# A segmented maximum and minimum in one 256-wide step, and straight code for the column loop of a graph network

## The reference, cut to what matters

```
for l in range(3):
    msg = concat([h[src], h[dst]]) @ Mw.T + Mb         # per edge, with self loops
    s1, s2 = segment_sum(msg, dst), segment_sum(msg * msg, dst)
    mx, mn = segment_max(msg, dst), segment_min(msg, dst)
    mean = s1 / deg
    var = relu(s2 / deg - mean * mean)
    std = sqrt(var + 1e-30)
    agg = concat([mx, mn, std, var])
    u = concat([h, agg, agg * (log(deg + 1) / 4), agg * (4 / log(deg + 1))]) @ Uw.T + Ub
    # batch norm, a product with mix_w, leaky relu, + h, layer norm, elu
```

## Time and profile before

| | |
|---|---|
| median of three runs | 3951.08 us (3942.02 to 3959.58) |
| the profiled execution | 3915.32 us |
| its span | 3913.5 us |
| mean granted TensorE clock | 0.785 |
| busy: PE, PEld, DVE, ACT, POOL | 63%, 35%, 57%, 18%, 32% |
| instructions in the trace | 50857 |
| bytes moved by DMA | 511.54 MB, mean 131 GB/s |

### The profile page before, as it was taken

The page is one execution under the profiler, slowest core; times in us unless marked ns, Lnnn a source line. Parts: engine busy times, 40 slices in busy tenths (PEclk is TensorE's granted clock), DMA queues, the critical chain, the costliest instruction groups (busy, mean ns, idle before and its releaser), DMA issues. The chain is left out here.

```text
span 3913.5 us, 50857 instructions
## 1 busy us (share of the span) xinstructions
PE 2472.3 (63%) x11996; PEld 1384.5 (35%) x11997; DVE 2233.6 (57%) x6995; ACT 692.3 (18%) x1557; POOL 1258.7 (32%) x1321
## 2 busy tenths in 40 slices
PE   6988879886968955455456654454448644544563
PEld 2444345743635532222224422222225322222242
DVE  6877766463353265555555645555556645555555
ACT  0235532411121030000001500000003300000112
POOL 3000000002000036666642155655640356555520
PEclk8999989997979977677678676766767867767785
DMA  3122366253523535444441144444430444444411
GB/s 109 50 93 109 142 210 230 99 206 124 176 81 138 176 100 179 159 163 159 138 145 40 53 160 144 160 155 135 157 113 1 141 136 160 154 134 158 153 43 45
DMA packets 152225, 511.54 MB, mean 131 GB/s; under 512 B 32194, under 2 KB 51552, under 8 KB 151248
## 3 DMA queue, kind: packets, MB, share of 16 engines
q1 hardware_dynamic: 94782, 350.03, 25.5%
q0 software_dynamic: 43536, 93.43, 8.6%
q10 hardware_dynamic: 13826, 67.12, 4.2%
HBM read 280.33 MB, written 230.13 MB: 130 GB/s over the span
## 5 line engine op out<-in xcount | busy, mean ns | idle before, releaser
L615 POOL DMA_INDIRECT rows_g<-a_dram,idx_now x1173 | 1133.3, 966 | 1566.8 <-DMA a_dram<-g 801.4
L1485 PE MATMUL psum<-hs,slab 128*128 128x384 bf16 x6600 | 1196.2, 341 | 166.2 <-issue 124.0
L1485 PEld LDWEIGHTS psum<-hs,slab 128*128 128x128 bf16 x6600 | 674.5, 102 | 711.2 <-issue 326.3
L1045 DVE SCALAR_TENSOR_TENSOR run<-run,mask_pt,rows_g 128x128 f32<-128x128 f32 x1170 | 405.6, 347 | 278.5 <-issue 224.7
L1048 DVE SCALAR_TENSOR_TENSOR run<-run,mask_pt,rows_g 128x128 f32<-128x128 f32 x1170 | 403.3, 345 | 34.6 <-issue 26.8
L1637 PE MATMUL psum<-identity,std_now 128*128 128x128 f32 x75 | 33.6, 448 | 598.1 <-ACT std_now L1341 512.9
L1432 PE MATMUL psum<-onehot_key,onehot_lane 128*128 128x512 bf16 (+1 forms) x1968 | 366.4, 343 | 60.9 <-issue 36.3
L726 DVE TENSOR_SCALAR onehot_key<-key_row,key_at 128x1600 bf16<-128x1600 f16 x492 | 310.2, 630 | 0.0
L1644 PE MATMUL psum<-w_U,vturned 128*128 128x384 f32 x150 | 119.2, 896 | 292.6 <-ACT vturned L1349 265.2
L1341 ACT ACTIVATE std_now<-var_now,eps 128x128 f32<-128x128 f32 x75 | 30.1, 401 | 1444.5 <-DVE var_now L1007 928.9
L1432 PEld LDWEIGHTS psum<-onehot_key,onehot_lane 128*128 128x128 bf16 x1968 | 160.4, 100 | 249.5 <-issue 55.0
(11 more groups left out here) (298 smaller groups left out, 3018.2 us busy)
## 6 DMA issues: line engine op xcount, KB each, us to landing
slab<-at_part SPq DMA_DIRECT2D x200, 800.0 KB
scan_dram<-run SPq DMA_DIRECT2D x291, 512.0 KB
at_part<-part_now ACTq DMA_DIRECT2D x50, 800.0 KB, 3.6
sums_dram<-run ACTq DMA_DIRECT2D x43, 576.0 KB, 2.9
rows_g<-a_dram,idx_now POOLq DMA_INDIRECT x1173
rows_g<-in_attr SPq DMA_DIRECT2D x43, 148.5 KB
a_dram<-g SPq DMA_DIRECT2D x3, 1600.0 KB, 7.7
agg<-sel_dram SPq DMA_DIRECT2D x3, 1600.0 KB
```

The lines of the kernel that those rows point to most:

```text
L615: nc.gpsimd.indirect_dma_start(rows_g[:, slot, j, :], None, a_dram, bass.IndirectOffsetOnAxis(ap=idx_now[:, slot, j:j + 1], axis=0)).then_ ...
L1045: V.scalar_tensor_tensor(at[:, 0:D], before[:, 0:D], mark, rows, ALU.add, ALU.max).then_inc(s_run, 1)
L1485: T_.matmul(ps[:, 0:3 * D], counts[:, k * P:(k + 1) * P], hs[:, k, at:at + 3, :].rearrange("p s f -> p (s f)"), start=(k == 0), stop=False ...
```

## The change

- POOL's, DVE's and ACT's column loops are written out as straight code; PE's and SP's stay register loops.
- A slot of rows_g is twice as wide. ACT writes the negated copy of each group's rows into its second half (one `mul` by -1 for the group). One maximum over 256 columns then yields the maximum and the negated minimum. The carry, the merge and the marks are adapted: everywhere max of negatives in place of min.
- Gathers take their indices straight from src_pt and wait for s_run; the index copies are gone.
- The sums of a block are reduced by one DVE instruction over both banks (`sums_of`); ACT squares the mean (`mean_squared`), DVE subtracts (`variance`), ACT applies relu and root (`deviations`). A node's own row enters the sums by two further matmuls of an identity matrix with hs, for each block.
- The two bias rows, which take_part added, are now added by a matmul of ones with L3_rows beside each `bu` product.
- The parts of a block are placed by `sums_at` and `take_at`. Small temporaries lie in slab[2] and in rows_g.

```diff
+def sums_at(b):
+    return min(4 * b + 3, 3 * b + 24)
+def take_at(b):
+    return sums_at(b) + (3 if b < NB - 2 else 2)
...
-        idx_now = sb("idx_now", [P, RING, Q], I32)
-        rows_g = sb("rows_g", [P, RING, Q, D], F32)
+        rows_g = sb("rows_g", [P, RING, Q, 2 * D], F32)
...
     # POOL
-                def gather(first, k):
-                    slot, n = k % RING, len(cols_of(k)) if isinstance(first, int) and first == 0 else Q
-                    pool.wait_ge(s_const, N_CONST)
-                    pool.wait_ge(s_idx, GT * l + first + (k + 1))
-                    pool.sem_inc(s_past, 1)
-                    for j in range(n):
+                for k in range(GT):
+                    slot = k % RING
+                    if k >= RING:
+                        pool.wait_ge(s_run, T * l + Q * (k - RING) + Q)
+                    elif l:
+                        pool.wait_ge(s_run, T * l)
+                        pool.wait_ge(s_st[slot], written_before(l, slot))
+                    for j, t in enumerate(cols_of(k)):
                         nc.gpsimd.indirect_dma_start(
-                            rows_g[:, slot, j, :], None, a_dram,
-                            bass.IndirectOffsetOnAxis(ap=idx_now[:, slot, j:j + 1], axis=0)).then_inc(s_gat[slot], 16)
+                            rows_g[:, slot, j, 0:D], None, a_dram,
+                            bass.IndirectOffsetOnAxis(ap=src_pt[:, t:t + 1], axis=0)).then_inc(s_gat[slot], 16)
...
     # DVE, sums and variance of a block
-                    for k in range(2):
-                        last = V.tensor_reduce(var_tmp[:, k, :], bank(2 + 2 * odd + k)[:, 0:3 * D].rearrange(
-                            "p (s f) -> p f s", s=3), AX.X, ALU.add)
+                    V.tensor_reduce(var_tmp[:, 2 * (b % 2):2 * (b % 2) + 2, :],
+                                    ps[:, :, 0:3 * D].rearrange("p k (s f) -> p k f s", s=3), AX.X,
+                                    ALU.add).then_inc(s_agg, 1)
+                def variance(b):
+                    n = NB * l + b
+                    dve.wait_ge(s_mean_sq, n + 1)
+                    if n:
+                        dve.wait_ge(s_var_now, n)
                     dve.wait_ge(s_agg, n + (NB * 5 + 4))
-                    (six more steps: + g, + ft, * rdeg, square, subtract, max with 0)
+                    V.scalar_tensor_tensor(var_raw[:], var_tmp[:, 2 * (b % 2) + 1, :], rdeg[:, b:b + 1], mean_sq[:],
+                                           ALU.mult, ALU.subtract).then_inc(s_var, 1)
...
     # DVE, take_part
-                    V.tensor_tensor(row(edge_sum, b), row(edge_sum, b), lrows[:, 0, :], ALU.add)
...
-                    V.tensor_tensor(u0, u0, lrows[:, 1, :], ALU.add).then_inc(s_vu, 1)
...
     # DVE, columns
-                        dve.wait_ge(s_run, steps - 1)
-                        V.scalar_tensor_tensor(at[:, 0:D], before[:, 0:D], mark, rows, ALU.add,
+                        dve.wait_ge(s_run, T * l + t)
+                        V.scalar_tensor_tensor(at, before, mask_pt[:, t:t + 1], rows, ALU.add,
                                                ALU.max).then_inc(s_run, 1)
-                        dve.wait_ge(s_run, steps)
-                        V.scalar_tensor_tensor(at[:, D:2 * D], before[:, D:2 * D], mark, rows,
-                                               ALU.subtract, ALU.min).then_inc(s_run, 1)
-                    (and the index copy of group k + RING)
+                for k in range(GT):
+                    columns(k)
+                    for b in range(NB):
+                        if sums_at(b) == k:
+                            sums_of(b)
+                        if sums_at(b) + 1 == k:
+                            variance(b)
+                        if take_at(b) == k:
+                            take_part(b)
                 take_part(NB - 1)
...
     # ACT
+                def mean_squared(b):
+                    n = NB * l + b
+                    act.wait_ge(s_agg, n + (NB * 5 + 4))
+                    if n:
+                        act.wait_ge(s_var, n)
+                    A.activation(mean_sq[:], var_tmp[:, 2 * (b % 2), :], ACT.Square,
+                                 scale=rdeg[:, b:b + 1]).then_inc(s_mean_sq, 1)
                 def deviations(b):
                     n = NB * l + b
-                    act.wait_ge(s_prime, 1)
+                    act.wait_ge(s_var, n + 1)
+                    act.wait_ge(s_vtr, n + 1)
+                    A.activation(var_now[:], var_raw[:], ACT.Relu).then_inc(s_var_now, 1)
                     act.wait_ge(s_var_now, n + 1)
                     A.activation(std_now[:], var_now[:], ACT.Sqrt, bias=eps[:, 1:2]).then_inc(s_std_now, 1)
...
-                with act.Fori(0, NB) as b:
-                    deviations(b)
-                    var_turned(b)
+                for k in range(GT):
+                    slot, n = k % RING, len(cols_of(k))
+                    act.wait_ge(s_gat[slot], gathered_before(l, slot) + 16 * Q * (k // RING) + 16 * n)
+                    A.mul(rows_g[:, slot, 0:n, D:2 * D], rows_g[:, slot, 0:n, 0:D], -1.0).then_inc(s_minus_rows, 1)
+                    for b in range(NB):
+                        if sums_at(b) + 1 == k:
+                            mean_squared(b)
+                        if sums_at(b) + 2 == k:
+                            deviations(b)
+                        if take_at(b) == k:
+                            var_turned(b)
+                deviations(NB - 1)
+                var_turned(NB - 1)
...
     # PE, after the 50 products of a block
+                if c >= CALLS:
+                    for ps, at in zip(banks, ats):
+                        T_.matmul(ps[:, 0:3 * D], identity16[:],
+                                  hs[:, ds(b, 1), at:at + 3, :].rearrange("p b s f -> p (b s f)"), start=False,
+                                  stop=False, skip_group_check=True)
...
     # PE, the products bu; the wait for s_lw stood behind them
+                pe.wait_ge(s_lw, 16 * len(LATER) * l + 16 * len(LATER))
+                both = weights["L3_rows"][0:1, 0:2, :].rearrange("p k f -> p (k f)")
...
                     T_.matmul(bank(6 + b % 2)[:, 0:2 * D], ft2[:, b * P:(b + 1) * P], weights["M"][:, D:3 * D],
-                             start=True, stop=True).then_inc(s_bu, 1)
-                pe.wait_ge(s_lw, 16 * len(LATER) * l + 16 * len(LATER))
+                             start=True, stop=False)
+                    T_.matmul(bank(6 + b % 2)[:, 0:2 * D], ones[0:1, :], both, start=False, stop=True).then_inc(s_bu, 1)
```

More of the change, by code:

```diff
@@ L964, in told @@
                     return V_LAYER * l + V_X3 + k
-                def take_indices(first, k):
-                    n = len(cols_of(k)) if isinstance(first, int) and first == 0 else Q
-                    V.tensor_copy(idx_now[:, k % RING, 0:n], src_pt[:, ds(Q * first + Q * k, n)]).then_inc(s_idx, 1)
-                if l:
-                    dve.wait_ge(s_run, 2 * T * l)
-                for k in range(RING):
-                    take_indices(0, k)
                 for b in range(NB):
@@ L1023, in take_part @@
[L1023 to L1035 removed]
+                    dve.wait_ge(s_take, 2 * n + 2)
@@ L1072, in _ @@
                 take_part(NB - 1)
                 dve.wait_ge(s_last_turned, l + 1)
[L1075 to L1077 removed]
+                for e in range(2):
+                    last = V.tensor_tensor_scan(carry_t[:, e, 1:P + 1], mask_turn[:], bank(0)[:, e * P:(e + 1) * P],
+                                                carry_t[:, e, 0:1], ALU.add, ALU.max)
```

145 lines of the change are left out of this document (47 added, 98 removed).

## The result

The changed kernel is **slower**: 4055.56 us median (4047.39 to 4060.08) against 3953.57 us of the kernel before beside it, ratio 1.0259 (95% interval 1.0229 to 1.029). The profiled execution has a span of 4050.1 us against 3913.5, so 136.6 us are to be explained. Forecast was 3775 us, a gain of 4.5%; the time lies above the range's 3990.

What follows compares the result with a forecast made beforehand. Bound: the column loop's convoy of POOL's gathers and engines that crawl meanwhile. 3915 - 403 (waits for DVE) + 240 (remaining stops) + 6 (bias) - 15 (loop ends) = 3743, times 1.009 gives 3775 us; range 3520 to 3990.

Steps and rivals of the forecast that it cites:

- convoy: PNA column loop: POOL runs through its ring of 16 gathers, the others slow down, POOL stops, they recover; 402.7 us idle.
- crawl: Column loop: slow stretch of the other engines while POOL gathers, 13 PE and 13 DVE instructions in 14 us.
- One stop in three blocks, 8 a layer, 24 x 10 = 240 us: Column loop: POOL's remaining waits for DVE after the change, 10 us each, 240 us against the 402.7 removed.
- one in two: Column loop: POOL stops in every second block, 360 us of waits, 3895 us in all; upper end of the forecast.
- crawl over 2.8 us after the last gather: First term of one 10 us POOL stop: the others' slow stretch ends 2.8 us after POOL's last gather.
- fewer instructions on DVE: Column loop: DVE's part, 34 instructions in 10 us, falls by half and register instructions go, so stops get rarer.
- ACT's queue chains everything to PE's answer: Rival, column loop: POOL runs dry in every block, 72 x 10 = 720 us, median 4260 us; chance 0.18.
- 6 us, 0 to 9.5 a layer: Bias products beside the 25 `bu` products: 2 us a layer on the path, 0 to 9.5; 6 us in the sum.
- the gathers do not wait for: Layer opening: gathers do not wait for the splits' end, so of 9.5 us of bias products 2 us count.
- 15 us saved: Layer ends, last gather to take_part: 12 to 14 us after narrower work; 15 us saved over three layers, 0 to 20.
- Durations and hidden work: Column loop: wide step 0.48 us, negation 0.6, joint reduction about 1, few table loads for 50; hidden beside POOL's gathers.
- POOL alone sets the pace: Rival, column loop: slow stretches vanish or pass without reaching POOL; 3503 us, median 3535; chance 0.22.

Runs made afterwards that it cites:

- a quarter of the gathers: Changed kernel without bias products, POOL gathering one column of four from a layer's fifth group on: 2740.4 us on a fast chip, 2831.0 us on another.
- the gate: Changed kernel, but POOL also waits, before group 4b + 5, for PE's count products of block b: 3775.6 us, ratio 0.9689 to the kernel before.
- half the products: Changed kernel, but PE leaves out 24 of the 48 count products of a block in the column loop: 3834.8 us, ratio 0.9846.
- late take_part: Changed kernel with take_part and the copy of the transposed variances five groups after the sums instead of three: 3876.5 us, ratio 0.9949.
- the run with the memsets: Changed kernel with twelve one-column memsets more on DVE behind each group, on a fast chip: 3452.2 us, ratio 1.0217 to the kernel before.

## Why the prediction was wrong

- **Where the bound lies** was read rightly: a convoy of POOL's gathers and a PE that crawls while they run, ended some time after POOL pauses. The run with a quarter of the gathers and the gate show it.
- **"One stop in three blocks, 8 a layer, 24 x 10 = 240 us" is the step that failed**, in the number of stops and in the price of one. POOL waited 513.6 us. The number was 36, 12 a layer: the prediction's own "one in two", for which it had 360 us and 3895. Three of them were the openings' (75 us together, see the bias products); the other 33 took 13.3 us each. Against the 240 us, nine stops more make 90 us, the price of the 33 makes 107 and the openings make 75.
- **In the price one term was too small: "crawl over 2.8 us after the last gather".** ACT's copy came 6.6 us after it on the mean of the 33 (4.9 to 7.6), because PE came back to its pace late and had products of the next block to end first; the rest of a stop took 6.6 us, for which the sum has 7.2. The 2.8 us were read from one cycle of the old first layer; in the old second and third layer the same distance was 4.1 and 3.3 us by median.
- **The number was argued from fewer instructions on DVE**, but the loops got shorter with fewer instructions on PE (half the products: 47 to 63 us less a layer), and those had grown by two a block. Straight code alone turned one stop a block into a short and a long one and cost 2.1%, which the prediction had at nothing.
- **The rival "ACT's queue chains everything to PE's answer"** had the right mechanism with twice the number (72 stops) and three quarters of the price. Its chain is worth 3.0%: late take_part, 0.9949 against 1.0259.
- **The bias products, "6 us, 0 to 9.5 a layer"**, were mis-sized: 41.6 us of PE more in a layer's opening, on the way to ACT's negations and so to POOL. Three errors in one: the price was taken from one row's mean where a product is two such instructions, at the faster clock, and "the gathers do not wait for" the splits was true of the old order only. Measured by leaving them out: 2.1 to 2.3%, some 85 us.
- **The loop ends, "15 us saved"**, cost 40 us in place of it (97.7 over the layers for 57.7). In the third layer ACT's copy comes 6.8 us after the last gather, and then take_part of three blocks follows, 10.7 us apart (starts at 3842.76, 3853.50 and 3864.08); in the old second layer, where the end took 14.9 us, it was two.
- **Durations and hidden work** were right: 0.48, 0.6, 0.95 for the joint reduction, and two table loads for 50.
- The rule of the Trainium skill ("Runtime: NRT & Kernel Launch", Instruction fetch mechanics) that unrolled code avoids fetches at branches brought nothing here: with straight code alone the kernel was 2.1% slower, and no run shows a gain from it.
- **"POOL alone sets the pace"**, 3503 us, is what the loop does on the fast chip (the run with the memsets); there it seems to hold for the kernel before as well, to judge by its 3380 us, and so brings no gain.

By ratios the parts are straight code +2.1%, arithmetic and order without the bias -1.6% (1.0047 against 1.021), bias products +2.1%. They add up to +2.6% by construction, each being the step from one run to the next. The runs come from different chips, and two that were repeated on another gave 1.0272 for 1.0259 and 0.9515 for 0.9468, so each part is good to half a percent at best. No run has the rest of the change with its register loops kept, so the price of straight code is that beside the old arithmetic.

**What stays open.** Why PE's instructions and semaphores are late on some chips while POOL issues indirect gathers. What the runs show is when: 9 to some 20 us after POOL's restart, and until some 2 to 7 us after it pauses. The thought of a store of records that fills came from the 200 and 215 instructions of two kernels; the 125 of the kernel before and the 268 with late take_part do not fit a fixed number, so it is a guess. The Trainium skill ("NOTIFIC — the notification-queue block", Register file and Interfaces) gives the block that writes the engines' records an internal FIFO of up to 511 records and says that its filling can stall an engine. No run here shows that FIFO; all times come from executions that were recorded, and the run meant to test it fell on a chip without the delay. Each chip was used in one session only, so what is fast may be the session and not the chip. Nor was it tried why straight code has a rhythm of two blocks, or what the changed kernel as it stands takes on a fast chip.

## What to carry to other kernels

Where two engines run in a convoy, count the stops and price each before pricing any instruction: here all edits of arithmetic and order were together worth 1.6%, one added wait 5.6%. Read the price from many of the stops, not from one cycle. A producer that runs ahead as far as its ring lets it can cost more than one that pauses for 3 us at a chosen point. And a small product beside another is priced from rows of both, at the clock of that stretch, with all that stands behind it in the queue it now leads to.

## What the runs showed of the hardware

- While POOL issues indirect gathers back to back, a semaphore of PE can arrive 8.4 us after its instruction (1690.55 to 1698.94, gated kernel), 2.4 us after the last gather, or even 25.5 us after it (1643.73 to 1669.21, half the products), 6.3 us after the last gather. With a quarter of the gathers ACT waits 0.9 us for it.
- In the cycle shown of the changed kernel the crawl sets in 18 us after POOL's restart, inside the second block of products (9 us in the kernel before, 20 us with late take_part); POOL's own pace of 1.25 to 1.29 us a gather does not suffer.
- A product of one row (1x128 weights, 256 f32 columns) takes as long as one of 128 rows: 676 and 670 ns an instruction, two to a product, at a granted clock of 0.50. The clock was 1.00 in the same stretch of the kernel before (1421 to 1434), where PE ran 27 matmuls in 13 us, and in that of the run without bias products (1420 to 1435).
- The kernel before, unchanged, took 3380.0 and 3386.5 us on two chips and 3899 to 3953 on the others, one session on each; in a trace from a fast one (the run with the memsets) ACT waits 8.3 us for PE's transposes in all three layers, against 905.0.
